# Graph attention over 128 graphs: the paired step loop written out in every engine's program

## The chip, the cores and the metric
One core of a Trainium2 chip runs the whole kernel. The metric is the device time of one execution in microseconds (us); lower is better.

## The reference
For each of 128 graphs with 128 nodes and 384 features: layer norm and ReLU, three projections with biases, attention with 12 heads of 32 that only sees linked nodes, and the residual.

```python
h = jnp.maximum(_layernorm(x, axis=-1), 0.0)
q, k, v = (_split_heads(h @ W + b) for W, b in ((Wq, bq), (Wk, bk), (Wv, bv)))
scores = jnp.einsum('bhqd,bhkd->bhqk', q, k) / sqrt(HD)
scores = jnp.where(adj_e > 0, scores + beta * adj_e, -9e15)
out = jnp.einsum('bhqk,bhkd->bhqd', softmax(scores), v)
return x + out.transpose(0, 2, 1, 3).reshape(B, N, D)
```

## The kernel before
**Steps.** Four graphs (512 tokens) make a step's work. Step s projects its four graphs to q, k and v and at the same time attends to the four graphs of step s - 1, so there are 33 steps: step 0 only projects, step 32 only attends. Buffers that live across a step are double, and the parity of the step (`par`) picks the half.

**Slots.** A step has 12 slots (4 graphs by 3 groups of 4 heads). In each slot TensorE makes the scores of the slot (`scores`, L439), turns the probabilities of the slot before (`turn_probs`, L447), runs its share of the projections (`project`, L427, and `turn`, L407, by the list PIECES), and multiplies the probabilities of two slots before by v (`values_of`, L462 to L464). ScalarE computes the exponentials (L513) and the high half of each split (L520, L528, L533, L538). VectorE adds the mask to the scores and finds their maximum (L631), and computes the low halves (L601, L611, L637). GpSimd normalises, splits v and adds x (L297 to L329).

**The spreads.** The scores want q and k of each head stacked in 96 partitions, so SyncE copies qT to q_st and kT to k_st by DMA (`spread`, L241 to L245): 12 DMAs for q once the low halves of q are there, and 12 for k once the low halves of k are there. The order of SyncE's work in a step is written by hand: the last store of the step before last, the load of x for the step after next, the q spread, one store, the load of the adjacency, the k spread, two stores. The first scores of step s + 1 wait for all 24 copies of step s (L435, L436).

**The loop.** Each engine has its own program. Steps 0 and 1 stand in it once, steps 2 to 29 are a loop of 14 turns over a pair of steps (`run_steps`, L200 to L209), and steps 30, 31 and 32 stand in it once again. Inside the loop the counts that a wait compares with, and the addresses of x, adj and out, come from registers that are worked out from the loop's counter; outside they are constants. `wait` (L195 to L198) leaves a wait out where its constant is zero or less; `has` (L211 to L213) says which parts a step has.

Of the kernel before, what the change touches and what calls it, by code (L numbers as in the profile page):

```python
# [21 lines left out]
def graph_attention_kernel(nc, x, adj, wq, bq, wk, bk, wv, bv, beta, out):  # L22
# [4 lines left out]
    CH = D // P  # L27
    G = 4
    STEPS = GRAPHS // G
    TOK = G * N  # L30
    SLOTS = G * CH
# [37 lines left out]
    PB = 3  # L69
# [9 lines left out]
    with ExitStack() as ctx:  # L79
# [115 lines left out]
        def wait(eng, s, value):  # L195

            if not isinstance(value, int) or value > 0:
                eng.wait_ge(s, value)  # L198

        def run_steps(eng, step):  # L200

            step(0, 0)
            step(1, 1)
            with eng.Fori(1, STEPS // 2 - 1) as pair:
                step(2 * pair, 0, True)
                step(2 * pair + 1, 1, True)
            step(STEPS - 2, 0)
            step(STEPS - 1, 1)
            step(STEPS, 0)  # L209

        def has(s, looped, first, last):  # L211

            return looped or first <= s <= last  # L213

# [8 lines left out]
        @block.sync  # L223
        def _(sp):
            for n, src in enumerate((wq, wk, wv)):
                sp.dma_start(w_raw[:, :, W_COLS[n]], src.rearrange("(c p) n -> p c n", p=P)).then_inc(w_in[n], 16)
                if n == 0:
                    for i, row in enumerate((bq, bk)):
                        sp.dma_start(b_row[:, i, :], rows_of(row)).then_inc(b_in, 16)
            sp.dma_start(bv_row[:], rows_of(bv)).then_inc(bv_in, 16)  # L230
            sp.dma_start(beta_col[:], beta.broadcast_to([P, 1])).then_inc(beta_in, 16)
            sp.dma_start(adjs[:], adj_v[0]).then_inc(adj_in, 16)
            sp.dma_start(xs[:, 1], x_v[1]).then_inc(x_in[1], 16)

            def spread(s, par, kind):

                n, src, dst, landed = (0, qT, q_st, q_in) if kind == "q" else (1, kT, k_st, k_in)
                wait(sp, scores_done, SLOTS * (s - 1))
                sp.nop(nofuse=True)
                wait(sp, qk_low, QK * s + CH * (n + 1))  # L240
                sp.nop(nofuse=True)  # L241
                for b, part in enumerate(BLOCKS[kind]):
                    for i in range(HPC):
                        sp.dma_start(dst[HD * b:HD * (b + 1), par, i],  # L244
                                     src[HD * i:HD * (i + 1), part]).then_inc(landed, 16)  # L245

            def store(s, j):

                wait(sp, added, G * s + j + 1)
                sp.nop(nofuse=True)  # L250
                sp.dma_start(out_v[s, j], on[:, j % 2, :]).then_inc(stored[j % 2], 16)

            def step(s, par, looped=False):
                proj, attend = has(s, looped, 0, STEPS - 1), has(s, looped, 1, STEPS)
                if has(s, looped, 2, STEPS):
                    store(s - 2, G - 1)
                if has(s, looped, 0, STEPS - 3):
                    sp.wait_ge(xb_done, G * (s + 1))
                    sp.wait_ge(normed, G * (s + 1))
                    sp.nop(nofuse=True)  # L260
                    sp.dma_start(xs[:, par], x_v[s + 2]).then_inc(x_in[par], 16)
                if proj:
                    spread(s, par, "q")
                if attend:
                    store(s - 1, 0)
                if has(s, looped, 0, STEPS - 2):
                    sp.wait_ge(mask_done, s + 1)
                    sp.nop(nofuse=True)
                    sp.dma_start(adjs[:], adj_v[s + 1]).then_inc(adj_in, 16)
                if proj:  # L270
                    spread(s, par, "k")
                if attend:
                    store(s - 1, 1)
                    store(s - 1, 2)
                if s is STEPS:
                    store(s - 1, 3)

            run_steps(sp, step)
            for b in range(2):
                sp.wait_ge(stored[b], 16 * GRAPHS // 2)  # L280

        @block.gpsimd
        def _(pool):
# [46 lines left out]

            def step(s, par, looped=False):
                proj, attend = has(s, looped, 0, STEPS - 1), has(s, looped, 1, STEPS)
                if proj:
                    add_bias(s, par, 0)
                    add_bias(s, par, 1)
                if has(s, looped, 2, STEPS):
                    add_x(s - 2, par, G - 1)
                if proj:
                    add_bias(s, par, 2)
                    add_bias(s, par, 3)  # L340
                if has(s, looped, 0, STEPS - 2):
                    rstd_of(s + 1)
                    normalise(s + 1, 1 - par)
# [11 lines left out]
                if proj:  # L355
                    split_v(s, par, 3)
                if s is STEPS:
                    add_x(s - 1, 1 - par, 3)
# [17 lines left out]
            pool.wait_ge(bv_in, 16)  # L376
            run_steps(pool, step)

        @block.tensor
        def _(pe):  # L380
            def bank_free(s, par, o, looped):

                if not looped and s == 0 and o < PB:
                    pe.wait_ge(h_low, o + 1)
                    return
                before, last, here = s, o - 1, par
                while True:
                    if last < 0:
                        before, last, here = before - 1, NB - 1, 1 - here
                    unit = UNITS[last]  # L390
                    runs = looped or before < STEPS - 1 or unit[0] != "turn"
                    if runs and BANK[here][last] == BANK[par][o]:
                        break
                    last -= 1
# [14 lines left out]

            def project(s, par, o, first, end, looped):  # L410

                kind, n = UNITS[o]
                bank = ps_p[BANK[par][o]]
                if first == 0:
                    bank_free(s, par, o, looped)
                if first == 0 and n == 0 and not looped and s == 0:
                    pe.wait_ge(w_low, ("q", "k", "v").index(kind) + 1)
# [48 lines left out]

            def step(s, par, looped=False):
                proj, attend = has(s, looped, 0, STEPS - 1), has(s, looped, 1, STEPS)
                ahead = has(s, looped, 0, STEPS - 2)
                drain = 2 if not looped and s == STEPS else 0  # L470
                for u in range(SLOTS + drain):
                    n = SLOTS * (s - 1) + u
                    if attend and u < SLOTS:
                        scores(s, par, u)
                    if attend and u - 1 < SLOTS and (looped or n >= 1):
                        turn_probs(n - 1, (u - 1) % 2)
                    if proj:
                        for o, first, end in PIECES[u]:
                            if UNITS[o][0] != "turn":
                                project(s, par, o, first, end, looped)  # L480
                            elif ahead:
                                bank_free(s, par, o, looped)
                                turn(s + 1, ps_p[BANK[par][o]], UNITS[o][1])
                    if attend and (looped or n >= 2):
                        late = u < 2
# [10 lines left out]
            for n in range(2):  # L496
# [3 lines left out]
                mm.then_inc(b_turned, 1)  # L500
            run_steps(pe, step)

        @block.scalar
        def _(act):
# [35 lines left out]

            def step(s, par, looped=False):
                proj, attend = has(s, looped, 0, STEPS - 1), has(s, looped, 1, STEPS)
                ahead = has(s, looped, 0, STEPS - 2)
                drain = 1 if not looped and s == STEPS else 0
                for u in range(SLOTS + drain):
                    n = SLOTS * (s - 1) + u
                    if attend and (looped or n >= 1):
                        p_high(n - 1, (u - 1) % 2)
# [21 lines left out]
            act.wait_ge(bias_set, 2)  # L570
            run_steps(act, step)

        @block.vector
        def _(dve):
# [80 lines left out]

            def step(s, par, looped=False):
                proj, attend = has(s, looped, 0, STEPS - 1), has(s, looped, 1, STEPS)
                ahead = has(s, looped, 0, STEPS - 2)
                drain = 3 if not looped and s == STEPS else 0
                for u in range(SLOTS + drain):  # L660
                    n = SLOTS * (s - 1) + u
                    ended, late, j = attend and u % CH == 2 and (looped or n > CH), u < CH, (u // CH - 1) % G
                    if attend and u < SLOTS:
                        bias_scores(s, par, u)
                    if ended:
                        invert_sums(s - 1 - late, j)
                    if attend and (looped or n >= 1) and u - 1 < SLOTS:
                        p_low(n - 1, (u - 1) % 2)
# [79 lines left out]
            dve.wait_ge(bias_set, 2)  # L748
            run_steps(dve, step)

# [21 lines left out]
```

## Time and profile before

| what | value |
|---|---|
| time before, median of 3 runs | 1184.02 us (1181.08 to 1184.4) |
| profiled execution, its own time | 1185.46 us |
| its span in the profile | 1183.7 us |
| instructions in the span | 38644 |
| PE busy | 1068.0 us (90%) |
| DVE busy | 955.6 us (81%) |
| ACT busy | 894.9 us (76%) |
| POOL busy | 570.2 us (48%) |
| mean granted TensorE clock | 0.97 |
| DMA packets, bytes | 91030, 138.14 MB |

The span runs from the first to the last instruction of the program. Busy shares are of the span. DMA-issuing and waiting instructions are not counted as busy, so SyncE has no busy time at all: what it does is seen in its own rows of the timeline and in the chain of waits. PE is TensorE's matmul side and PEld its weight loads. The granted clock is a share of 2.4 GHz.

### The profile page before, as it was taken

To read this page: it belongs to the slowest core of one execution; us is meant where nothing else is said; L and a number is where in the kernel's file an instruction comes from. 1 tells how busy PE (TensorE), PEld (TensorE's weight loads), DVE (VectorE), ACT (ScalarE), POOL (GpSimd) and SP (SyncE) were. 2 spreads that over 40 slices of the span, in tenths; PEclk is the share of its full clock that TensorE was granted. 3 is DMA by queue.
4 is the path that set the end of the run, shared out by engine and by line. 5 is a ranking of instruction groups with operands and counts; after the bars stand their busy time and mean duration, and the time that the engine had idled before them with its cause. 6 is when DMAs were issued, how large, how long until landed. Compare 5 with 4: busy or idle time off the path is not lost.

```text
span 1183.7 us, 38644 instructions
## 1 busy us (share of the span) xinstructions
PE 1068.0 (90%) x10959; PEld 903.9 (76%) x10959; DVE 955.6 (81%) x4343; ACT 894.9 (76%) x2343; POOL 570.2 (48%) x756
## 2 busy tenths in 40 slices
PE   4699889999999999999999999999999999999975
PEld 2588777787787888778788777878877777888764
DVE  6488778888887888888888888888888888888764
ACT  2387777887787787778788787778878877887764
POOL 4634535444544545454454455445445545444421
PEclk9899999999999999999999999999999999999975
DMA  4444335544444544434554444455444445543330
GB/s 142 116 106 115 108 98 143 136 114 120 114 110 123 143 129 114 120 107 109 137 142 117 116 117 116 114 137 136 119 121 114 116 114 141 136 116 97 79 91 28
DMA packets 91030, 138.14 MB, mean 117 GB/s; under 512 B 15600, under 2 KB 66288, under 8 KB 90864
## 3 DMA queue, kind: packets, MB, share of 16 engines
q1 hardware_dynamic: 90336, 135.85, 42.7%
q14 instruction: 149, 1.22, 0.3%
q10 hardware_dynamic: 528, 0.79, 0.2%
q8 instruction: 17, 0.28, 0.1%
HBM read 35.91 MB, written 25.17 MB: 52 GB/s over the span
## 4 chain that ended last, share of the span: by engine, by line
PE 57%; SPq 13%; issue 11%; DVE 10%; DMA 4%; ACT 1%; POOL 1%; DVEq 1%; POOLq 0%; ACTq 0%
PE ps_p L427 34%; SPq L244 13%; PE ps_t L447 9%; PE ps_s L439 6%; DMA k_st<-kT 4%; DVE biased L631 4%; DVE kT L611 2%; PE ps_o L462 2%; PE ps_o L463 2%; PE ps_o L464 2%; DVE on L652 1%; DVE hT L601 1%; PE ps_p L407 1%; ACT probs L513 1%; DVE neg_max L631 1%
## 5 line engine op out<-in xcount | busy, mean ns | idle before, releaser
L631 DVE CUSTOM_DVE_ANT_0 biased<-ps_s,mask 128x128 f32<-128x128 f32 x1536 | 351.5, 284 | 177.6 <-PE ps_s L439 163.5
L513 ACT ACTIVATE probs<-biased,neg_max 128x128 f32<-128x128 f32 x1536 | 487.1, 391 | 6.0 <-DVE neg_max L631 6.0
L427 PE MATMUL ps_p<-hT,w 128*128 128x512 f32 x1728 | 473.7, 414 | 5.2 <-DVE qT L611 4.3
L538 ACT ACTIVATE pT<-ps_t 128x512 f16<-128x512 f32 x384 | 229.4, 597 | 239.7 <-PE ps_t L447 238.8
L427 PEld LDWEIGHTS ps_p<-hT,w 128*128 128x128 f32 x1728 | 312.6, 193 | 63.2 <-DVE qT L611 4.8
L637 DVE TENSOR_TENSOR pT<-ps_t,pT 128x512 f16<-128x512 f32 x384 | 256.9, 669 | 17.2 <-ACT pT L538 16.8
L447 PE MATMUL ps_t<-ident,probs 128*128 128x128 f32 x1536 | 241.1, 281 | 16.2 <-ACT probs L513 15.7
L329 POOL TENSOR_TENSOR on<-on,xb 128x384 f32<-128x384 f32 x128 | 128.7, 1005 | 260.1 <-DVE on L652 257.8
L427 PE MATMUL ps_p<-w,hT 128*128 128x384 f32 x1152 | 243.9, 347 | 0.0
L439 PE MATMUL ps_s<-k_st,q_st 96*128 96x128 f16 x1536 | 151.0, 221 | 52.2 <-DMA k_st<-kT 46.6
L427 PEld LDWEIGHTS ps_p<-w,hT 128*128 128x128 f32 x1152 | 193.5, 189 | 2.7
L321 POOL CAST v<-v_f 128x384 f16<-128x384 f32 x128 | 64.9, 507 | 267.2 <-ACT v_f L528 249.9
L462 PEld LDWEIGHTS ps_o<-v,pT 128*128 128x128 f16 x1536 | 123.8, 97 | 81.2 <-issue 51.3
L447 PEld LDWEIGHTS ps_t<-ident,probs 128*128 128x128 f32 x1536 | 165.9, 144 | 21.7 <-ACT probs L513 21.3
L462 PE MATMUL ps_o<-v,pT 128*128 128x33 f16 x1536 | 160.9, 181 | 1.1 <-DVE pT L637 1.1
L463 PE MATMUL ps_o<-v,pT 128*128 128x33 f16 x1536 | 155.7, 178 | 0.0
L464 PE MATMUL ps_o<-v,pT 128*128 128x32 f16 x1536 | 155.7, 177 | 0.0
L439 PEld LDWEIGHTS ps_s<-k_st,q_st 96*128 96x128 f16 x1536 | 90.7, 97 | 56.3 <-issue 56.3
L314 POOL TENSOR_TENSOR xb<-xs,bv_row 128x384 f32<-128x384 f32 x128 | 127.8, 1021 | 0.0
L463 PEld LDWEIGHTS ps_o<-v,pT 128*128 128x128 f16 x1536 | 126.1, 97 | 1.2
L631 DVE DVE_READ_ACCUMULATOR2_ANT neg_max<- 128x1 f32 x1536 | 126.5, 82 | 0.0
L464 PEld LDWEIGHTS ps_o<-v,pT 128*128 128x128 f16 x1536 | 124.1, 96 | 0.0
(59 smaller groups left out, 1073.5 us busy)
## 6 DMA issues: line engine op xcount, KB each, us to landing
q_st<-qT SPq DMA_DIRECT2D x384, 96.0 KB, 2.2
k_st<-kT SPq DMA_DIRECT2D x384, 96.0 KB, 2.1
out<-on SPq DMA_DIRECT2D x128, 192.0 KB, 1.9
xs<-in_x SPq DMA_DIRECT2D x31, 768.0 KB, 4.7
adjs<-in_adj SPq DMA_DIRECT2D x32, 256.0 KB, 2.8
xs<-in_x ACTq DMA_DIRECT2D x1, 768.0 KB, 7.3
k_st<-in_L_gnn_Wq SPq DMA_DIRECT2D x1, 576.0 KB, 5.5
k_st<-in_L_gnn_Wk SPq DMA_DIRECT2D x1, 576.0 KB, 9.3
```

The source lines that it names most:

```text
L244: sp.dma_start(dst[HD * b:HD * (b + 1), par, i], src[HD * i:HD * (i + 1), part]).then_inc(landed, 16)
L329: pool.tensor_tensor(on[:, j % 2, :], on[:, j % 2, :], xb[:, par, j, :], ALU.add).then_inc(added, 1)
L427: mm = pe.matmul(dst, stationary, moving, start=m == 0, stop=m == MMS - 1)
L439: mm = pe.matmul(ps_s[u % 2][:, i * N:(i + 1) * N], q_st[0:STACK, 1 - par, i, c, j * N:(j + 1) * N], k_st[0:STACK, 1 - par, i, c, j * N:(j ...
L447: mm = pe.transpose(ps_t[:, i * N:(i + 1) * N], probs[:, odd, i, :], ident[:])
L462: pe.matmul(o, high, first, start=True, stop=False)
L463: pe.matmul(o, low, first, start=False, stop=False)
L464: mm = pe.matmul(o[:, 0:HD], high, second, start=False, stop=True)
L513: act.activation(probs[:, odd, i, :], biased[:, odd, i, :], ACT.Exp, bias=neg_max[:, odd, i:i + 1], scale=-1.0).then_inc(exp_done, 1)
L538: act.activation(pT[:, odd, 0], ps_t[:].rearrange("p (h q) -> p h q", q=N), ACT.Copy).then_inc(p_high_done, 1)
L631: dve.tensor_tensor_reduce(out=biased[:, odd, i, :], in0=ps_s[odd][:, i * N:(i + 1) * N], in1=mask[:, 1 - par, u // CH, :], scale=-1.0, sc ...
L637: dve.tensor_tensor(pT[:, odd, 1], ps_t[:].rearrange("p (h q) -> p h q", q=N), pT[:, odd, 0], ALU.subtract).then_inc(p_low_done, 1)
```

## The change
`run_steps` no longer emits a loop. It calls each engine's `step` 33 times with plain integers, so every engine's program holds all steps one after the other, in the same order and with the same work. The `looped` arguments, which told a step that it stood in the loop, go, and so do the register arithmetic and the branches. All waits compare with constants.

```diff
-            if not isinstance(value, int) or value > 0:
+            if value > 0:
                 eng.wait_ge(s, value)
 
-        def run_steps(eng, step):
-
-            step(0, 0)
-            step(1, 1)
-            with eng.Fori(1, STEPS // 2 - 1) as pair:
-                step(2 * pair, 0, True)
-                step(2 * pair + 1, 1, True)
-            step(STEPS - 2, 0)
-            step(STEPS - 1, 1)
-            step(STEPS, 0)
-
-        def has(s, looped, first, last):
-
-            return looped or first <= s <= last
+        def run_steps(step):
+
+            for s in range(STEPS + 1):
+                step(s, s % 2)
...
-            def step(s, par, looped=False):
-                proj, attend = has(s, looped, 0, STEPS - 1), has(s, looped, 1, STEPS)
-                if has(s, looped, 2, STEPS):
+            def step(s, par):
+                proj, attend = 0 <= s <= STEPS - 1, 1 <= s <= STEPS
+                if 2 <= s <= STEPS:
                     store(s - 2, G - 1)
...
-            run_steps(sp, step)
+            run_steps(step)
...
-                    if attend and (looped or n >= 2):
+                    if attend and n >= 2:
                         late = u < 2
                         values_of(s - 1 - late, par if late else 1 - par, (u - 2) % SLOTS, n - 2, u % 2)
```

The other engines' `step`, and `bank_free` and `project` on TensorE, lose their `looped` argument in the same way.

## Rows read from the trace of the kernel before

**Rows 1.** The page: busy shares, and the chain that ended last by engine.
```profile
PE 1068.0 (90%) x10959; PEld 903.9 (76%) x10959; DVE 955.6 (81%) x4343; ACT 894.9 (76%) x2343; POOL 570.2 (48%) x756
...
PE 57%; SPq 13%; issue 11%; DVE 10%; DMA 4%; ACT 1%; POOL 1%; DVEq 1%; POOLq 0%; ACTq 0%
```

**Rows 2.** Timeline, PE, first scores of steps 4, 5, 6, 14, 30, 31: start, length, [idle before].
```profile
166.23 0.39 PE L439 MATMUL ps_s<-k_st,q_st 96*128 96x128 f16 x4 [3.16 <-DMA k_st<-kT]
...
202.17 0.40 PE L439 MATMUL ps_s<-k_st,q_st 96*128 96x128 f16 x4 [1.30 <-DMA k_st<-kT]
...
236.84 0.39 PE L439 MATMUL ps_s<-k_st,q_st 96*128 96x128 f16 x4 [1.59 <-DMA k_st<-kT]
...
514.55 0.40 PE L439 MATMUL ps_s<-k_st,q_st 96*128 96x128 f16 x4 [1.69 <-DMA k_st<-kT]
...
1069.65 0.38 PE L439 MATMUL ps_s<-k_st,q_st 96*128 96x128 f16 x4 [1.12 <-issue]
...
1104.79 0.38 PE L439 MATMUL ps_s<-k_st,q_st 96*128 96x128 f16 x4 [2.08 <-issue]
```

**Rows 3.** Timeline, SP: the k spreads of steps 1, 2, 3, 5, 6, 29, 30, 31.
```profile
83.46 7.52 SPq L244 DMA_DIRECT2D k_st<-kT  x12
...
117.82 8.89 SPq L244 DMA_DIRECT2D k_st<-kT  x12
...
155.03 9.37 SPq L244 DMA_DIRECT2D k_st<-kT  x12
...
227.22 7.50 SPq L244 DMA_DIRECT2D k_st<-kT  x12
...
262.18 7.50 SPq L244 DMA_DIRECT2D k_st<-kT  x12
...
1060.49 7.50 SPq L244 DMA_DIRECT2D k_st<-kT  x12
...
1094.67 8.29 SPq L244 DMA_DIRECT2D k_st<-kT  x12
...
1131.26 7.50 SPq L244 DMA_DIRECT2D k_st<-kT  x12
```

**Rows 4.** Chain of waits inside the k spread of step 2: start, length, what.
```profile
120.29 1.97 SPq L244
```

**Rows 5.** DMA queues, 120.2 to 121.9: packets, MB, share of 16 engines' time.
```profile
q8 instruction: 1, 0.02, 6.0%
```

**Rows 6.** DMA queues: instruction packets in 0 to 167, 167 to 1069, 1069 to 1183.7.
```profile
q8 instruction: 9, 0.15, 0.4%
...
q14 instruction: 126, 1.03, 0.4%
...
q8 instruction: 8, 0.13, 0.5%
```

**Rows 7.** DMA queues: instruction packets, k spreads of steps 3 and 29; all of step 30.
```profile
q8 instruction: 1, 0.02, 1.2%
...
q14 instruction: 1, 0.01, 0.3%
...
q8 instruction: 3, 0.05, 0.6%
```

**Rows 8.** Busy by stretch: start of steps 4 (3.4 us), 5 to k spread, 3 to k spread, all of 30.
```profile
167.20:170.60 3.40, 3.40 (x23) 2.42 (x23) 1.97 (x9) 1.76 (x5) 0.26 (x1) 0.50 0.01 4
...
202.17:227.22 25.05, 25.05 (x259) 21.01 (x260) 22.51 (x104) 19.78 (x53) 11.61 (x16) 1.00 0.41 113
...
128.54:155.03 26.49, 26.49 (x259) 22.03 (x260) 22.57 (x104) 19.77 (x53) 10.30 (x14) 0.94 0.37 101
...
1069.70:1104.80 35.10, 32.32 (x343) 27.56 (x344) 29.53 (x136) 27.66 (x73) 18.39 (x25) 1.00 0.38 101
```

**Rows 9.** Timeline, DVE: first maximum after the scores of steps 6 and 7.
```profile
238.15 0.29 DVE L631 CUSTOM_DVE_ANT_0 biased<-ps_s,mask 128x128 f32<-128x128 f32 x1 [1.70 <-PE ps_s L439]
...
272.19 0.29 DVE L631 CUSTOM_DVE_ANT_0 biased<-ps_s,mask 128x128 f32<-128x128 f32 x1 [0.77 <-PE ps_s L439]
```

More of the change, by code:

```diff
@@ L251, in store @@
                 sp.dma_start(out_v[s, j], on[:, j % 2, :]).then_inc(stored[j % 2], 16)
-            def step(s, par, looped=False):
-                proj, attend = has(s, looped, 0, STEPS - 1), has(s, looped, 1, STEPS)
-                if has(s, looped, 2, STEPS):
+            def step(s, par):
+                proj, attend = 0 <= s <= STEPS - 1, 1 <= s <= STEPS
+                if 2 <= s <= STEPS:
                     store(s - 2, G - 1)
-                if has(s, looped, 0, STEPS - 3):
+                if 0 <= s <= STEPS - 3:
                     sp.wait_ge(xb_done, G * (s + 1))
@@ L265, in step @@
                     store(s - 1, 0)
-                if has(s, looped, 0, STEPS - 2):
+                if 0 <= s <= STEPS - 2:
                     sp.wait_ge(mask_done, s + 1)
@@ L274, in step @@
                     store(s - 1, 2)
-                if s is STEPS:
+                if s == STEPS:
                     store(s - 1, 3)
-            run_steps(sp, step)
+            run_steps(step)
             for b in range(2):
@@ L329, in add_x, with step @@
                 pool.tensor_tensor(on[:, j % 2, :], on[:, j % 2, :], xb[:, par, j, :], ALU.add).then_inc(added, 1)
-            def step(s, par, looped=False):
-                proj, attend = has(s, looped, 0, STEPS - 1), has(s, looped, 1, STEPS)
+            def step(s, par):
+                proj, attend = 0 <= s <= STEPS - 1, 1 <= s <= STEPS
                 if proj:
@@ L335, in step @@
                     add_bias(s, par, 1)
-                if has(s, looped, 2, STEPS):
+                if 2 <= s <= STEPS:
                     add_x(s - 2, par, G - 1)
@@ L340, in step @@
                     add_bias(s, par, 3)
-                if has(s, looped, 0, STEPS - 2):
+                if 0 <= s <= STEPS - 2:
                     rstd_of(s + 1)
@@ L356, in step @@
                     split_v(s, par, 3)
-                if s is STEPS:
+                if s == STEPS:
                     add_x(s - 1, 1 - par, 3)
@@ L376, in _, with bank_free @@
             pool.wait_ge(bv_in, 16)
-            run_steps(pool, step)
+            run_steps(step)
         @block.tensor
         def _(pe):
-            def bank_free(s, par, o, looped):
-                if not looped and s == 0 and o < PB:
+            def bank_free(s, par, o):
+                if s == 0 and o < PB:
                     pe.wait_ge(h_low, o + 1)
@@ L390, in bank_free @@
                     unit = UNITS[last]
-                    runs = looped or before < STEPS - 1 or unit[0] != "turn"
+                    runs = before < STEPS - 1 or unit[0] != "turn"
                     if runs and BANK[here][last] == BANK[par][o]:
@@ L408, in turn, with project @@
                 mm.then_inc(h_turned, 1)
-            def project(s, par, o, first, end, looped):
+            def project(s, par, o, first, end):
                 kind, n = UNITS[o]
@@ L414, in project @@
                 if first == 0:
-                    bank_free(s, par, o, looped)
-                if first == 0 and n == 0 and not looped and s == 0:
+                    bank_free(s, par, o)
+                if first == 0 and n == 0 and s == 0:
                     pe.wait_ge(w_low, ("q", "k", "v").index(kind) + 1)
@@ L465, in values_of, with step @@
                 mm.then_inc(pv_done, 1)
[L467 to L470, printed above, removed]
+            def step(s, par):
+                proj, attend = 0 <= s <= STEPS - 1, 1 <= s <= STEPS
+                ahead = 0 <= s <= STEPS - 2
+                drain = 2 if s == STEPS else 0
                 for u in range(SLOTS + drain):
@@ L474, in step @@
                         scores(s, par, u)
-                    if attend and u - 1 < SLOTS and (looped or n >= 1):
+                    if attend and u - 1 < SLOTS and n >= 1:
                         turn_probs(n - 1, (u - 1) % 2)
@@ L479, in step @@
                             if UNITS[o][0] != "turn":
-                                project(s, par, o, first, end, looped)
+                                project(s, par, o, first, end)
                             elif ahead:
-                                bank_free(s, par, o, looped)
+                                bank_free(s, par, o)
                                 turn(s + 1, ps_p[BANK[par][o]], UNITS[o][1])
-                    if attend and (looped or n >= 2):
+                    if attend and n >= 2:
                         late = u < 2
@@ L500, in _ @@
                 mm.then_inc(b_turned, 1)
-            run_steps(pe, step)
+            run_steps(step)
         @block.scalar
@@ L539, in p_high, with step @@
                                ACT.Copy).then_inc(p_high_done, 1)
[L541 to L544, printed above, removed]
+            def step(s, par):
+                proj, attend = 0 <= s <= STEPS - 1, 1 <= s <= STEPS
+                ahead = 0 <= s <= STEPS - 2
+                drain = 1 if s == STEPS else 0
                 for u in range(SLOTS + drain):
                     n = SLOTS * (s - 1) + u
-                    if attend and (looped or n >= 1):
+                    if attend and n >= 1:
                         p_high(n - 1, (u - 1) % 2)
@@ L570, in _ @@
             act.wait_ge(bias_set, 2)
-            run_steps(act, step)
+            run_steps(step)
         @block.vector
@@ L654, in scale_out, with step @@
                                   ALU.mult).then_inc(scaled, 1)
[L656 to L659, printed above, removed]
+            def step(s, par):
+                proj, attend = 0 <= s <= STEPS - 1, 1 <= s <= STEPS
+                ahead = 0 <= s <= STEPS - 2
+                drain = 3 if s == STEPS else 0
                 for u in range(SLOTS + drain):
                     n = SLOTS * (s - 1) + u
-                    ended, late, j = attend and u % CH == 2 and (looped or n > CH), u < CH, (u // CH - 1) % G
+                    ended, late, j = attend and u % CH == 2 and n > CH, u < CH, (u // CH - 1) % G
                     if attend and u < SLOTS:
@@ L666, in step @@
                         invert_sums(s - 1 - late, j)
-                    if attend and (looped or n >= 1) and u - 1 < SLOTS:
+                    if attend and n >= 1 and u - 1 < SLOTS:
                         p_low(n - 1, (u - 1) % 2)
@@ L748, in _ @@
             dve.wait_ge(bias_set, 2)
-            run_steps(dve, step)
+            run_steps(step)
 _INS = ["x", "adj", "L0_gnn_Wq", "L0_gnn_bq", "L0_gnn_Wk", "L0_gnn_bk", "L0_gnn_Wv", "L0_gnn_bv", "L0_gnn_beta"]
```

## The prediction
> **What bounds the kernel now.** I read the page first, then the chain of waits, then SyncE's and TensorE's rows of the timeline, then the DMA queues by stretch. On the page TensorE is busy 90% of the span and no other engine passes 81%, but 13% of the chain lies in SyncE's issuing and 4% in DMA landings [rows 1]. So TensorE alone does not set a step's length. The timeline shows what does: the first scores of every step wait for the last copies of k_st, 1.30 us in one step and 1.59 us in the next [rows 2]. Those copies start as soon as the last low half of k is done, their 12 issues take 7.50 us [rows 3], and the last lands some 2 us later. A step is therefore a cycle of three terms. From the first scores to the first issue of the k spread TensorE sets the pace: 227.22 - 202.17 = 25.05 us, fully busy [rows 2, 3, 8]. The 12 issues are 7.50 us. From their end to the next first scores is 236.84 - 234.72 = 2.12 us. What TensorE does after k's projection (v, turns, the last slots) lies beside the second and third term and has the idle time shown as slack. The order that follows: time saved on TensorE's late part is worth nothing, and any delay of SyncE during the k spread comes through in full.
>
> **What the change removes.** The 26 steps 4 to 29 run on loop turns 2 to 14 and take (1069.65 - 166.23) / 26 = 34.75 us each [rows 2]. A step with constants and without a branch stands in the trace too: step 30. Its first term is 1094.67 - 1069.65 = 25.02 us [rows 2, 3]. The way from the end of the issues to the next scores, where those scores wait on a constant, is 1069.65 - (1060.49 + 7.50) = 1.66 us [rows 2, 3]; the loop's 2.12 us above has the register arithmetic before the wait, and in odd steps a landing that falls together with the branch. With 7.50 us of issues that makes 25.02 + 7.50 + 1.66 = 34.18 us for a step that nothing disturbs.
>
> Where the difference comes from: after the branch back, VectorE begins the first maximum 238.15 - 236.84 = 1.31 us after the scores and the step's first term is 262.18 - 236.84 = 25.34 us, against 25.05 us in the odd step [rows 2, 3, 9]. That is 0.3 us for a turn here. VectorE had been idle for 1.70 us against 0.77 us [rows 9]; the trace shows 126 instruction packets on queue 14 inside the looped part [rows 6], so the other engines refetch their loop bodies on each turn. All this goes. 26 x 34.18 = 888.7 us; add 1.45 us (worked out below) because step 4 still begins at the low clock after step 3; against 903.4 us now the gain is 13.3 us. Steps 2 and 3 lose their register arithmetic and the landing at the branch, some 0.7 us in all. **Gain: 14.0 us.** Steps 0, 1, 30, 31 and 32 keep their code.
>
> **What the change adds.** No operation, no wait, no DMA of the kernel's own; nothing is moved past another queue. What it adds is instruction fetch by TensorE. Queue 8 fetches 9 packets in the first 167 us and 8 in the last 115 us, and has no row at all from 167 to 1069 us [rows 6]: once the pair of steps has been run, TensorE's program stays on the chip. Written out, it is fetched throughout. The packets are 0.15 MB / 9 = 16 KB each. Step 30, written out, holds 3 [rows 7].
>
> Does a fetch cost anything? The k spread of step 2 takes 8.89 us in place of 7.50, step 3's 9.37 and step 30's 8.29 [rows 3]. In the chain of step 2 it is a single issue that takes 1.97 us [rows 4], and in just that stretch queue 8 moves one packet, for 6.0% x 16 engines x 1.7 us = 1.6 us [rows 5]. The spread of step 3 holds one queue 8 packet, the undisturbed spread of step 29 only a small one of queue 14 [rows 7]. So I read it thus: while a 16 KB instruction packet occupies a DMA engine, SyncE can't finish an issue that needs that engine. The price is 1.39, 1.87 and 0.79 us in the k spreads; q spreads show 0.6 to 1.2 us, but there SyncE afterwards waits for k anyway, so those are hidden. I take 1.1 us per disturbed k spread; bounds 0.6 and 1.6 us (step 3's excess holds another 0.3 us at the branch).
>
> The second part of the price is the clock. The first scores that waited 3.16 us (step 4), 2.08 us (step 31) and 1.69 us (step 14) were each followed by a stretch at granted clock 0.50, that is 1.2 GHz; those that had waited 1.59 us or less were not [rows 2, 8]. In a step with such a stretch the first term is 155.03 - 128.54 = 26.49 us for step 3 and 1131.26 - 1104.79 = 26.47 us for step 31, where step 5 has 25.05 [rows 2, 3, 8]: 1.45 us more. A written-out step idles 1.12 us before its scores [rows 2]; with 0.6 to 1.6 us on top it idles 1.7 to 2.7 us, which is where all the rows with a low clock lie. Sum per disturbed spread: 1.1 + 1.45 = 2.55 us, bounds 2.05 and 3.0 us.
>
> **How many spreads.** Of the k spreads of steps 1, 2, 3, 30 and 31, all in code run for the first time, 3 are disturbed [rows 3]. From the rate: 3 packets over 34.2 us [rows 7], and a spread open for 7.5 us, gives 3 x 7.5 / 34.2 = 0.66. As a step has 343 matmuls and as many loads plus some waits [rows 8], which is no whole number of packets, the packets wander through the step and do not stay outside the spread. I take the lower of the two, 0.6: 26 steps x 0.6 = 16 disturbed spreads in steps 4 to 29; bounds 13 (one in two) and 20 (three in four). **Loss: 16 x 2.55 = 40.8 us.**
>
> The Trainium skill speaks against this sum. "Runtime: NRT & Kernel Launch", section "Instruction fetch mechanics", says that the sequencer streams a long program with a mostly hidden cost at block boundaries, while a taken branch out of the window forces a fetch and is why full unrolling is preferred. Its second half agrees with the late VectorE after the branch [rows 9]; by its first half the loss would be about nothing and the result the 14 us gain. The row that decides for me is the issue of 1.97 us [rows 4]: the fetch is hidden from TensorE, but not from SyncE.
>
> **The sum.** 1183.7 (span) - 14.0 + 40.8 = 1210.5 us of span. The profiled execution takes 1.8 us more than its span and lies 1.4 us above the median, so the forecast for the median is 1184.0 + 26.8 = 1211 us, 2.3% slower.
>
> **Rivals.**
> 1. Faster. The fetches of steps 4 to 29 fall mostly outside the k spreads, or an issue waits for them only in the first pass, for another reason that goes away. The place is SyncE's L244, the price is nothing, and what remains is the 14 us: 1170 us. It decides as soon as fewer than 14 / 2.55 = 5 or 6 of the 26 spreads are hit. For it: in steps 1 and 31 no spread is disturbed. Against it: the long issue of step 2 and its packet lie together to a fraction of a us [rows 4, 5], and step 30 was disturbed too, after the loop had run 14 times [rows 3]. The page of the Trainium skill named above would give this time too.
> 2. The stalls come, but the clock stays up, because the idle time is spread otherwise: 16 x 1.1 = 17.6 us, less 14.0, gives 1188 us. Against it: the wait of 1.69 us was enough for a low stretch [rows 2].
> 3. Heavier: three spreads in four are hit at 3.0 us: 60 - 14 = 46 us, 1230 us, or beyond it if the other engines' packets delay landings too. For it: in step 3 the excess was 1.87 us. Against it: queue 14's packet in the spread of step 29 cost nothing.
> 4. Nothing changes: gain and loss cancel at about 6 spreads, or the program's fetch is too rare to matter and the branches too. 1184 us.
>
> **How the numbers follow.** My forecast, with 13 to 20 spreads at 2.05 to 3.0 us, reaches from 1184 - 14 + 26.7 = 1197 to 1230 us: chance 0.66. Rival 1 has 0.11, rival 2 0.13, rival 3 beyond 1230 us 0.06, rival 4 0.04. The predicted time is 1211 us. The range takes in rival 2 and ends at the forecast's upper bound, 1187 to 1231 us, and leaves out rivals 1, 3 and 4. A difference of 0.3% (3.6 us) is about what a measurement of this kernel can tell. Faster by more: 0.11. Within it: 0.05 (rival 4 and the lower edge of rival 2). Slower: 0.84.
>
> **What would show it.** Queue 8 should have 90 to 95 packets of 16 KB where it had 17. SyncE's k spreads should be of two kinds, 7.5 us and 8.1 to 9.4 us, with 13 to 20 of the latter in steps 4 to 29, each holding a queue 8 packet, and each followed by first scores that idled over 1.7 us and a stretch at clock 0.50. Undisturbed steps should take 34.2 us, and VectorE's first maximum should come 0.7 us after the scores in all steps. The page should show more idle time of PE before ps_s L439, a lower mean clock, and a larger SPq share of the chain. I am wrong if the long issues do not appear beside the packets, if they appear and the next scores do not move (then SyncE had slack that I don't see), or if undisturbed steps stay at 34.7 us.

## The result and the profile after

| | before | after |
|---|---|---|
| median | 1183.23 us (1181.08 to 1184.4, 6 runs) | 1200.82 us (1195.5 to 1201.92, 6 runs) |
| span of the profiled execution | 1183.7 us | 1200.0 us |
| steps 4 to 29 | 903.4 us | 922.2 us |
| queue 8 packets in all, in steps 4 to 29 | 17, 0 | 88, 71 |
| mean granted clock | 0.97 | 0.96 |

The ratio is 1.0139, 95% interval 1.0114 to 1.0163: slower by 1.4%, inside the range of 1187 to 1231 us and 10 us below the forecast of 1211 us.

The page after: busy shares, instruction packets by queue, and the chain by engine:

```profile
span 1200.0 us, 33777 instructions
...
PE 1077.0 (90%) x10959; PEld 912.0 (76%) x10959; DVE 963.0 (80%) x4343; ACT 894.5 (75%) x2343; POOL 570.6 (48%) x756
...
q8 instruction: 88, 1.44, 0.5%
q14 instruction: 86, 0.70, 0.2%
...
PE 80%; issue 9%; DVE 6%; SPq 1%; POOL 1%; ACT 0%; DMA 0%; DVEq 0%; POOLq 0%; ACTq 0%
```

There are 4867 fewer instructions, the register arithmetic and the branches, and the kernel is slower all the same. The chain is a trap here. It had 13% of SyncE's issuing before [rows 1] and has 1% now, though SyncE delays the steps more. The rows of the next fences show where it is lost: for the idle time of the first scores the profile names no releaser but "issue", as it did in steps 30 and 31 of the kernel before [rows 2], and the chain goes on along TensorE. The timeline shows the dependence all the same. SyncE's k spreads of steps 6 to 14, and the first scores of steps 7 to 13, with [idle before]:

```profile
257.02 8.87 SPq L234 DMA_DIRECT2D k_st<-kT  x12
...
294.06 8.57 SPq L234 DMA_DIRECT2D k_st<-kT  x12
...
331.00 7.83 SPq L234 DMA_DIRECT2D k_st<-kT  x12
...
365.55 7.56 SPq L234 DMA_DIRECT2D k_st<-kT  x12
...
399.78 8.48 SPq L234 DMA_DIRECT2D k_st<-kT  x12
...
434.98 8.93 SPq L234 DMA_DIRECT2D k_st<-kT  x12
...
472.17 9.03 SPq L234 DMA_DIRECT2D k_st<-kT  x12
...
509.49 7.50 SPq L234 DMA_DIRECT2D k_st<-kT  x12
...
543.66 7.95 SPq L234 DMA_DIRECT2D k_st<-kT  x12
```

```profile
267.58 0.38 PE L429 MATMUL ps_s<-k_st,q_st 96*128 96x128 f16 x4 [2.53 <-issue]
...
304.53 0.38 PE L429 MATMUL ps_s<-k_st,q_st 96*128 96x128 f16 x4 [2.44 <-issue]
...
340.54 0.38 PE L429 MATMUL ps_s<-k_st,q_st 96*128 96x128 f16 x4 [1.50 <-issue]
...
374.75 0.38 PE L429 MATMUL ps_s<-k_st,q_st 96*128 96x128 f16 x4 [1.18 <-issue]
...
409.96 0.38 PE L429 MATMUL ps_s<-k_st,q_st 96*128 96x128 f16 x4 [2.15 <-issue]
...
445.57 0.49 PE L429 MATMUL ps_s<-k_st,q_st 96*128 96x128 f16 x4 [2.56 <-issue]
...
482.89 0.38 PE L429 MATMUL ps_s<-k_st,q_st 96*128 96x128 f16 x4 [2.69 <-issue]
```

The first scores follow the end of the spread at a fixed distance, 267.58 - (257.02 + 8.87) = 1.69 us and 374.75 - (365.55 + 7.56) = 1.64 us. Where the spread of the step before is 7.5 us, TensorE idles 1.2 us; where it is 8.5 to 9.0 us, 2.2 to 2.7 us. In the looped kernel every spread from step 4 to 29 was 7.5 us [rows 3 show steps 5, 6 and 29]. Instruction packets during two of the spreads after, the long one of step 6 (257.02 to 265.89) and the short one of step 9 (365.56 to 373.1):

```profile
q8 instruction: 1, 0.02, 1.1%
...
q14 instruction: 1, 0.01, 0.5%
```

The first row is the long spread's only one, the second the short spread's: a queue 8 packet there, a small one of queue 14 here. This holds for all 26 spreads of steps 4 to 29: the 17 with a queue 8 packet take 7.88 to 9.03 us, the nine without one 7.50 to 7.83 us. TensorE's clock, as busy time by stretch (PE, PEld, DVE, ACT, POOL, then granted clock): just after the scores of steps 7 and 11, and the first terms of steps 6 and 7:

```profile
268.30:271.60 3.30, 3.30 (x18) 2.32 (x18) 2.12 (x11) 1.76 (x5) 1.10 (x2) 0.50 0.00 0
410.20:413.60 3.40, 3.40 (x36) 2.87 (x34) 2.57 (x13) 1.93 (x6) 1.99 (x3) 1.00 0.11 37
231.99:257.02 25.03, 25.03 (x259) 20.99 (x260) 22.67 (x105) 19.78 (x53) 11.73 (x16) 1.00 0.41 114
267.58:294.06 26.48, 26.48 (x259) 21.97 (x260) 22.67 (x104) 19.84 (x53) 10.37 (x14) 0.94 0.36 100
```

Step 7 began after 2.53 us of idle time and ran its first 3.4 us at 1.2 GHz; its first term is 26.48 us instead of 25.03. Step 11 began after 2.15 us of idle time and stayed at 2.4 GHz.

**The account of steps 4 to 29.** 26 undisturbed steps would be 26 x 34.18 = 888.7 us. 17 of the 26 k spreads are long and each has a queue 8 packet; added up, their rows exceed 7.50 us by 16.1 us, 0.95 us each. The other nine exceed it by 0.45 us together. Ten steps have a stretch at clock 0.50: 10 x 1.45 = 14.5 us. That is 919.8 us; the remaining 2.4 us of 922.2 are landings up to 0.6 us later than usual and first terms up to 0.2 us longer. Steps 0 to 3 took 3.0 us less than before and what follows step 29 took 0.5 us more: 18.8 - 3.0 + 0.5 = 16.3 us, the difference of the spans.

### The profile page after: what moved, and what is told of

It is laid out like the page before. It is cut to its first block, busy times and chain, and to the rows that moved or that the text cites. A ratio compares the mean times of both kernels' runs of the same rounds, so it can differ in the third digit from the quotient of the medians.

```text
span 1200.0 us, 33777 instructions
## 1 busy us (share of the span) xinstructions
PE 1077.0 (90%) x10959; PEld 912.0 (76%) x10959; DVE 963.0 (80%) x4343; ACT 894.5 (75%) x2343; POOL 570.6 (48%) x756
## 4 chain that ended last, share of the span: by engine, by line
PE 80%; issue 9%; DVE 6%; SPq 1%; POOL 1%; ACT 0%; DMA 0%; DVEq 0%; POOLq 0%; ACTq 0%
PE ps_p L417 47%; PE ps_t L437 13%; PE ps_s L429 8%; PE ps_o L452 3%; PE ps_o L453 3%; PE ps_o L454 3%; PE ps_p L397 3%; DVE biased L621 2%; DVE pT L627 2%; DVE hT L591 2%; SPq L234 1%; POOL on L319 0%; ACT probs L503 0%; DMA k_st<-kT 0%; POOL v L313 0%
## 5 line engine op out<-in xcount | busy, mean ns | idle before, releaser
L417 PE MATMUL ps_p<-hT,w 128*128 128x512 f32 x1728 | 483.5, 420 | 4.1 <-DVE qT L601 3.3
L417 PEld LDWEIGHTS ps_p<-hT,w 128*128 128x128 f32 x1728 | 319.0, 196 | 64.2 <-DVE qT L601 3.7
```

The costliest lines, as they stand in the source:

```text
L417: mm = pe.matmul(dst, stationary, moving, start=m == 0, stop=m == MMS - 1)
```

## The experiments

All are timed against the kernel before. In the first group, `run_steps(eng, step, looped)` chooses the loop or the written-out steps for each engine by itself.

**TensorE looped, the others written out.**

```diff
-            run_steps(sp, step)
+            run_steps(sp, step, False)
...
-            run_steps(dve, step)
+            run_steps(dve, step, False)
```

> TensorE keeps its loop, all other engines are written out. Theory A (TensorE's 16 KB instruction packets block SyncE's issues): queue 8 is silent from about 165 to 1060 us, all k spreads of steps 4 to 29 take 7.5 us, the steps take 34.3 to 34.5 us (TensorE's own register arithmetic before the wait for the copies stays), the median is 1184 - 14 + 28 x 0.15 = 1174 us (1170 to 1178). Theory B (the long issues come from SyncE's own program, or the other engines', being run for the first time in every step): two in three k spreads stay long, and the time is 1195 us or more.

Measured: 1180.62 us, ratio 0.9973 (0.9963 to 0.9983). Instruction packets between 167 and 1060 us:

```profile
q14 instruction: 71, 0.58, 0.2%
```

There is no row of queue 8, and no spread from step 5 to 29 takes more than 7.81 us. Long issues need TensorE's packets, although SyncE's program is written out. Theory B falls. The gain was a third of what I expected, though: 3.3 us against the kernel before in place of 10, and 1180.62 us lies outside the 1170 to 1178 us that I gave. Undisturbed steps take 34.4 us as forecast, but late landings after steps 7, 14 and 21 and three stretches at the low clock (in steps 4, 8 and 15) bring the mean of steps 4 to 29 to 34.7 us.

**TensorE alone written out.** The edit is `run_steps(pe, step, False)` and no other.

> Only TensorE is written out, the other engines keep their loops. Theory A: 15 to 20 of the 26 k spreads of steps 4 to 29 are long, each with a queue 8 packet, and the late VectorE after each branch is there as well: 1202 to 1210 us. Theory B: k spreads of 7.5 us, 1180 to 1184 us.

Measured: 1211.06 us, ratio 1.0239 (1.0216 to 1.0261). The long spreads are there with the other engines looped, so TensorE's program alone brings the loss: 16 of the 26 spreads of steps 4 to 29 hold a queue 8 packet, and 14 of these take 7.82 to 8.85 us. The median is 10 us above the kernel after and 1 us above the top of what I had expected. What the 10 us are is only in part seen, for the traced execution is the fastest of the four (1205.72 us). The late VectorE is back in it: step 10 begins a new turn, with its first scores at 378.27 us and VectorE's first maximum at 380.33 us, 2.06 us later. In the looped kernel this distance is 1.31 [rows 9] to 1.93 us at the start of the turns from step 6 to 28. Here it is 1.50 to 2.06 us in the six of these steps whose scores had waited 1.1 to 1.4 us, and 0.65 to 0.86 us in the six whose scores had waited 2.5 to 2.7 us: late scores hide the refetch, as I read it. VectorE, timeline:

```profile
380.33 0.29 DVE L634 CUSTOM_DVE_ANT_0 biased<-ps_s,mask 128x128 f32<-128x128 f32 x1 [1.99 <-issue]
```

**SyncE alone looped, the others written out.**

> Only SyncE keeps its loop. Theory A: as the written-out kernel, 1197 to 1204 us, with 15 to 20 long k spreads in steps 4 to 29. Theory B in its form for SyncE's own program: 1168 to 1180 us.

Measured: 1195.93 us, ratio 1.0111 (1.0085 to 1.0138), and long spreads in two of three steps as in the kernel after. Whether SyncE's own program is written out or not makes no difference that these runs can tell: the interval overlaps with that of the kernel after. The median lies 1 us below the lower bound that I gave.

**TensorE kept busy while it waits.** The written-out kernel with ten matmuls ahead of the wait for the copies.

```diff
                 if u == 0:
+                    wait(pe, biased_done, HPC * (n - 1))
+                    for i in range(10):
+                        pe.matmul(ps_s[0][:, 0:N], ident[:], ident[:], start=True, stop=True)
                     pe.wait_ge(q_in, 16 * 3 * HPC * s)
```

> The written-out kernel with ten extra matmuls of ident with ident in each step just before the wait for the copies, into the bank that the first scores then overwrite; they take 1.1 us in which TensorE otherwise idles. Theory: the low clock follows the long idle time before the scores. The long issues stay (about 17 in steps 4 to 29), the stretches of 3.4 us at clock 0.50 in steps 4 to 29 (ten in the written-out kernel) go to 0 to 3, and the time falls by 1.45 us for each, to 1186 us (1183 to 1192). Rival: the clock falls for another reason, ten stretches stay and the time stays at 1200 us. Other rival: the extra matmuls delay the scores where no issue was long, and the time rises above 1203 us.

Measured: 1196.62 us, ratio 1.0111 (1.0095 to 1.0128). Busy time from 90 to 1140 us, with the mean granted clock third from the end, of this kernel and then of the kernel after:

```profile
90.00:1140.00 1050.00, 1028.42 (x10772) 887.77 (x10771) 877.30 (x4011) 821.63 (x2169) 514.18 (x677) 1.00 0.45 119
```

```profile
90.00:1140.00 1050.00, 974.87 (x10111) 828.12 (x10109) 873.20 (x3991) 817.64 (x2159) 515.42 (x676) 0.98 0.44 118
```

The clock behaved as expected, no low stretch is left in steps 2 to 31, but the time missed its range of 1183 to 1192 us. The effect of the other rival was there too, if smaller than its 1203 us: ten of these matmuls take 2.2 us, not 1.1, because each is two passes of 0.11 us, so every step was at least 35.2 us long. My size for the filling was wrong, and the gain from the clock was spent on it.

**The same with four.**

> The written-out kernel with four extra matmuls before the wait for the copies instead of ten; four take 0.9 us (ten took 2.2 us and filled more than the 1.1 us that were idle, so undisturbed steps took 35.2 us). Theory: the low stretches stay away as with ten, undisturbed steps take 34.2 us again, disturbed ones their long issue more; 1200 - 10 x 1.45 = 1185 us (1181 to 1190). Rival: with less filled the clock falls again, 1195 to 1200 us.

Measured: 1186.36 us, ratio 1.0032 (1.0020 to 1.0045). The step that was disturbed still has its long issue, but its scores idle less and the clock stays at 1.00. SyncE's spreads of steps 4 and 5 and the first scores between them:

```profile
186.62 8.66 SPq L234 DMA_DIRECT2D k_st<-kT  x12
...
221.99 8.29 SPq L234 DMA_DIRECT2D k_st<-kT  x12
```

```profile
196.97 0.38 PE L432 MATMUL ps_s<-k_st,q_st 96*128 96x128 f16 x4 [1.32 <-issue]
```

The first term of step 5 is 221.99 - 196.97 = 25.02 us. Against the kernel after this is 14.5 us less by median, the ten stretches at 1.45 us. The spreads cost the same in both: added up over steps 4 to 29 they exceed 7.50 us by 16.4 us here and by 16.5 us in the kernel after. The clock's share of the loss is thereby shown.

**Packets beside the spread, packets in the spread.** The strongest test keeps the work and the number of packets and moves only their place. A step of TensorE has 705 instructions. 63 waits that are always met bring it to 768. The packets, three a step, then come at nearly the same places in every step, as the traces of both kernels show; a count ahead of step 0 chooses the places.

```diff
                     mm = pe.matmul(dst, stationary, moving, start=m == 0, stop=m == MMS - 1)
+                    i = PROJ.index(UNITS[o]) * MMS + m
+                    if 2 <= s <= STEPS - 2 and (i + 1) * 63 // 90 > i * 63 // 90:
+                        pe.wait_ge(consts_set, 3)
+                        pe.nop(nofuse=True)
...
+            for i in range(37):
+                pe.wait_ge(consts_set, 3)
+                pe.nop(nofuse=True)
             run_steps(step)
```

> The written-out kernel with 63 waits that are always met spread over TensorE's projections of each step, so that a step has 768 instructions, three whole instruction packets, and with 37 more ahead of step 0, which put the packets of every step at about 0, 11 and 22 us after its first scores, outside the k spread (25.0 to 32.5 us). Theory (what costs is where in the step TensorE's packets fall): no long issue in a k spread from step 2 on, though there are more packets than in the written-out kernel; steps of 34.2 to 34.4 us, no stretch at the low clock from step 2 to the last; 1165 us (1160 to 1172), faster than both kernels. Rival (the number of packets costs, or the extra instructions do): 1200 us or more.

> The same kernel and the same 63 waits a step, but 145 instead of 37 ahead of step 0: the packets come at about 6, 18 and 28.5 us after the first scores, the last inside the k spread of every step. Theory: a long issue in all 29 k spreads of steps 2 to 30, 0.95 us each on average as in the written-out kernel, and about six in ten of them followed by the low clock at 1.45 us: 1165 + 29 x (0.95 + 0.87) = 1218 us (1200 to 1235). Rival (place does not matter): the same time as with 37, within 5 us.

Measured: 1169.17 us, ratio 0.9885 (0.9855 to 0.9915), with 37, and 1219.62 us, ratio 1.0325 (1.0289 to 1.0361), with 145. The page counts 95 packets on queue 8 with 37 and 96 with 145. SyncE's k spreads of steps 5 to 7, and the longest single issue of a k spread (min/median/max ns), with 37:

```profile
220.96 7.53 SPq L234 DMA_DIRECT2D k_st<-kT  x12
...
255.17 7.51 SPq L234 DMA_DIRECT2D k_st<-kT  x12
...
289.62 7.51 SPq L234 DMA_DIRECT2D k_st<-kT  x12
```

```profile
L234 SPq DMA_DIRECT2D k_st<-kT x384: 507/592/822, 47.9 to 1123.2; - x192
```

and with 145, steps 5 to 7:

```profile
234.20 8.04 SPq L234 DMA_DIRECT2D k_st<-kT  x12
...
268.93 8.20 SPq L234 DMA_DIRECT2D k_st<-kT  x12
...
305.39 8.04 SPq L234 DMA_DIRECT2D k_st<-kT  x12
```

In the kernel after the same row of issues reads

```profile
L234 SPq DMA_DIRECT2D k_st<-kT x384: 507/592/2117, 47.7 to 1154.5; - x192
```

With 145 the packets come at about 9, 20 and 29 us after the first scores. All 29 spreads of steps 2 to 30 are long, by 0.79 us on average, and 13 stretches at the low clock follow; with 37 there are two, and no spread of these steps takes more than 7.78 us. The traced executions differ by 46.1 us of span, the medians by 50.5 us. Of the 46.1 us, 9.1 us lie in step 0 (the first scores of step 1 come at 66.14 us against 57.08), whose k spread already starts 9.0 us later; this is the price of the waits put ahead of it and has nothing to do with the spreads. The spreads account for 29 x 0.79 = 22.8 us and eleven more low stretches for 11 x 1.45 = 16.0 us. That is 47.9 us, 1.8 us too much, because the kernel with 37 has small delays of its own, 1.1 us in the spreads of steps 4 to 29 and 1.1 us more in landings than the other. Without the 9.1 us the place of the packets is worth 37 us by the traces and 41 us by the medians, over 3% of the kernel. Their number by itself costs little: 95 packets in the right place give a kernel that is faster than the one with 17.

**TensorE looped and kept busy.** The first experiment's kernel with four matmuls ahead of the wait.

> TensorE in its loop, the others written out, and the four extra matmuls. The kernel without the four had three low stretches in steps 4 to 30. Theory: these go, 1180.6 - 3 x 1.45 = 1176 us (1173 to 1179). Rival: the extra matmuls cost as much as they save, 1179 to 1183 us.

Measured: 1172.07 us, ratio 0.9907 (0.9882 to 0.9932). This is 1 us below the range that I gave and 8.6 us below the first experiment, of which the three stretches explain 4.4. The rest fits TensorE's register arithmetic: from the end of the issues to the scores it takes 1.64 to 1.70 us in undisturbed steps instead of 1.83, so some 0.15 us in each of 28 looped steps, 4.2 us. That the arithmetic is now done beside the four matmuls is how I read it; no run separates it.

**Both edits together.** Always-met waits for TensorE, cut to 47 and 21, and the four matmuls.

> Both edits together: the written-out kernel with four extra matmuls before the wait for the copies, and the always-met waits cut to 47 a step and 21 ahead of step 0, since the four matmuls are 16 instructions, so that a step again has 768. Theory: no long k spread beside a packet from step 2 to 30, and the low stretches after steps 7 and 14 of the kernel with 63 waits go too, so 1169 - 2 x 1.45 = 1166 us (1163 to 1169). Rival: the packets have moved by the new count and meet the k spread again, 1180 us or more.

Measured: 1201.72 us, ratio 1.0154 (1.0139 to 1.0169): a miss, the rival's way. The packets did stay in place from step to step, but at about 12, 25 and 32.4 us after the first scores, where the kernel with 63 waits has them at about 1.5, 14 and 23.5 us. Two now fall at the edges of the spread. Timeline, SP, k spreads of steps 9, 10 and 23:

```profile
367.89 8.35 SPq L234 DMA_DIRECT2D k_st<-kT  x12
...
402.93 8.97 SPq L234 DMA_DIRECT2D k_st<-kT  x12
...
862.60 7.50 SPq L234 DMA_DIRECT2D k_st<-kT  x12
```

The spread of step 23 has no long issue and is late all the same. The first scores of step 24 and, for 870 to 871 us, the packets of queue 8 and the last issue of k_st with its time to landing:

```profile
872.60 0.38 PE L436 MATMUL ps_s<-k_st,q_st 96*128 96x128 f16 x4 [0.98 <-issue]
```

```profile
q8 instruction: 1, 0.02, 6.8%
...
k_st<-kT SPq DMA_DIRECT2D x1, 96.0 KB, 3.0
```

From the end of the issues to the scores it is 872.60 - 870.10 = 2.50 us instead of 1.64, and the landing takes 3.0 us where the page of this kernel has 2.2 us by median. This one counted, the same is seen after 12 of the 29 spreads of steps 2 to 30, 2.42 to 3.00 us each, always with a queue 8 packet that begins within 0.5 us of the end of the issues. So a packet costs in two ways, by a long issue or, at the end of the spread, by a late landing; my price had the first only. Three stretches at the low clock are left too, in steps 5, 28 and 29, after waits of 1.76, 1.85 and 1.89 us behind the four matmuls. In the kernel that has the matmuls alone no such wait was longer than 1.55 us, so its clock stayed up with the waits kept short, and the matmuls are no cure where they get longer.

The run confirms what a packet in the spread does, and shows that its place could not be worked out from my count: the two kernels have the same number of instructions per step and ahead of step 2, though in this one the first scores stand 16 instructions later in the step. Why the four matmuls move the packets stays open.

## Why the prediction was right, and where it was off

**What bounds a step** held as written: undisturbed steps after are 25.02 + 7.56 + 1.64 = 34.2 us, and a long spread moves the next scores by its full excess.

**The gain of 14.0 us** was not measured by itself. The nearest is the kernel with the packets beside the spread: its undisturbed steps are 34.15 to 34.25 us, as the sum has them. By median it lies 14 us below the kernel before, but that the number is the same is chance. In steps 4 to 29 it takes 895.6 us, 7.9 us less than before and 6.9 us above 26 x 34.18, of which two low stretches are 2.9 us and the rest is late landings and small delays; the other half of its gain lies outside, mostly in the long spreads of steps 2, 3 and 30 and what follows them, which the forecast left in. The first experiment shows a limit that the sum lacked. It assumed that the landings of a written-out kernel are never disturbed. They are, now and then, and beside a queue 14 packet: after step 7 of the kernel with 37 waits the scores idle 2.01 us though the spread is 7.51 us, and one queue 14 packet lies in the 1.2 us after its last issue. No run moves these packets, so that they are the cause is not shown. Rivals 1 and 4 said nothing of such landings either.

Two smaller readings were off as well. The branch was priced at 0.3 us a turn from step 6, one of its cheaper places; over the undisturbed steps that begin a turn the first term is 25.47 us on average, 0.4 us more than in the odd steps (the gain itself was taken from the whole of steps 4 to 29 and did not need this). And steps 0 to 3 became 3.0 us shorter, where I had 0.7 us.

**The loss of 40.8 us** has three factors. The number of spreads was 16 by forecast and 17 by count. The issue was 1.1 us by forecast and 0.95 us by measurement. The clock term is the one that was mis-sized: I charged 1.45 us to every disturbed spread, because every wait of 1.69 us or more in the trace before was followed by a low stretch, but those were few rows. In steps 4 to 29 the scores that followed the 17 long spreads had waited 1.65 to 2.69 us, and only ten of them were followed by one: the waits of 2.34 us (after step 20) and 2.46 us (after step 15) were not, the wait of 1.78 us (after step 22) was. The length of the wait does not decide alone. 17 x 0.95 + 10 x 1.45 = 30.6 us in place of 40.8 is the whole distance between forecast and result. That nothing is left over is luck: some 3.3 us of late landings, small delays and the steps behind step 29 were in no term, while 2.3 us more in steps 0 to 3 and the 1.45 us charged to step 4, which began at the full clock, came back.

**Rival 1**, with the page of the Trainium skill that calls the fetch mostly hidden ("Runtime: NRT & Kernel Launch", "Instruction fetch mechanics"): the fetch is hidden from TensorE here, as the page says; it is busy for 25.03 us of the 25.03 us of step 6's first term, in the row above, in which two queue 8 packets arrive. It is not hidden from another engine's DMA issues. The same section's remark on branches agrees with the first experiments: written out, the other engines gain, 3 us with TensorE looped and 10 us with TensorE written out, though their register arithmetic goes with the branches.

**Rival 2**, a clock that stays up, gave 1188 us. It did not happen in the kernel after, but it is what the kernel with four matmuls brings about: 1186 us.

**What I said would show it** mostly did: 88 packets for 90 to 95, and spreads of two kinds, 17 long ones for 13 to 20, of which four stay under the 8.1 us that I gave as their least. VectorE's first maximum comes 0.56 us after the scores, earlier than the 0.7 us. The stretch at clock 0.50 after each long spread did not appear, as told. A larger share of SyncE in the chain did not appear either: all kernels with TensorE written out have 1%. A wait on constants is not the whole reason, for TensorE looped with the four matmuls has 1% too, and without them 17%.

## What to carry to other kernels

One engine's instruction fetch can hold up another engine's DMAs. That they meet in a DMA engine that both need is how I read it; no row names the engine. Writing a loop out is free only if no other engine issues DMAs on the path while the longer program is fetched, so look for single issues of two or three times the usual length, for landings that come late behind the last issue, and for an instruction packet beside them. If an engine's loop runs without a single packet of its own, as TensorE's does here [rows 6], keep that loop and write out the others; or put the packets where no transfer is awaited. And before adding up a clock penalty for each wait, count how many waits of that length were not followed by one.

## What the runs showed of the hardware

- In the k spreads of the kernel after, an issue that meets a 16 KB instruction packet takes 0.8 to 2.1 us instead of 0.59 us (longest 2.117 us). Packets of queue 14, of half the size, mostly leave the issues alone (the longest beside one is 0.91 us, in step 8); late landings, by up to 0.6 us, lie beside them.
- Where a 16 KB packet begins at the end of a spread, the next scores come 0.8 to 1.4 us late without a long issue beside it: 12 times in steps 2 to 30 of the kernel with both edits.
- TensorE's program for two steps, about 1470 instructions, is run 13 times (steps 4 to 29) with no packet on queue 8 [rows 6], while queue 14 moves 126 packets for the other engines in that time.
- 63 always-met waits per step inside TensorE's projections cost nothing that shows: its first term stayed at 25.02 us. 108 more ahead of step 0 made step 0 9.1 us longer.
- The granted clock fell to 1.2 GHz for 3.4 us after 10 of the 17 long waits in steps 4 to 29 of the kernel after, and after none in steps 2 to 31 where four matmuls of 0.9 us in all were put ahead of the wait, although these left waits of up to 1.55 us. With the same four matmuls it did fall after waits of 1.76 to 1.89 us, in the kernel with both edits.
